# First attention of a fused decoder: rounded inputs scaled by ScalarE, value product and output product one tile sooner, orders set anew

## The reference

```
x = x + attn(layernorm(x))            # layer 0: 16 heads of 32, 4 key/value heads, causal
ln_out = layernorm(x) * ln_w + ln_b   # input of the second attention, for its q, k, v and cross q
y  = clip(ln_out / in_scale, -448, 448)       # in_scale: 512 values for each of the four uses
y  = fp8_e4m3(bf16(y))                        # rounded, used in the next products
```

## Time and profile before

| | us |
|---|---|
| median of 3 runs | 3635.28 (3631.49 to 3635.35) |
| profiled execution, its own time | 3634.33 |
| its span | 3632.6 |
| busy in the span: PE / DVE / ACT / POOL | 3308.4 / 2482.3 / 1673.9 / 855.2 |

### The profile page before, as it was taken

How to read it: one execution, slowest core, us unless ns; L and a number is a source line. 1 busy time by engine, 2 the same in 40 slices (tenths; PEclk the granted TensorE clock), 3 DMA queues, 4 the chain that set the end, 5 groups by cost and what they waited for, 6 DMA issues and landing times. The chain is left out here.

```text
span 3632.6 us, 54605 instructions
## 1 busy us (share of the span) xinstructions
PE 3308.4 (91%) x18088; PEld 2670.3 (74%) x18088; DVE 2482.3 (68%) x6423; ACT 1673.9 (46%) x4003; POOL 855.2 (24%) x915
## 2 busy tenths in 40 slices
PE   5654999997899999999999997999989979998999
PEld 4443887785687787778778775888878757766887
DVE  5997888887566666766666657799765555558333
ACT  5443445444434344444434432688637655542222
POOL 1222444443222222332222223100133310000000
PEclk9877999999999999999999997999999989999999
DMA  6113002002000000110000005899920124333000
GB/s 224 23 23 75 0 0 70 0 0 89 20 21 28 19 21 28 66 43 21 28 19 21 28 0 207 314 407 393 348 80 2 47 105 123 118 102 105 11 10 21
DMA packets 113584, 296.12 MB, mean 82 GB/s; under 512 B 37920, under 2 KB 42016, under 8 KB 107664
## 3 DMA queue, kind: packets, MB, share of 16 engines
q1 hardware_dynamic: 107264, 276.39, 21.6%
q0 software_dynamic: 6160, 17.67, 1.6%
HBM read 251.65 MB, written 41.68 MB: 81 GB/s over the span
## 5 line engine op out<-in xcount | busy, mean ns | idle before, releaser
L40 PE MATMUL bank<-w,cross_ctx_part 128*125 128x512 f32 x1536 | 517.3, 418 | 8.1 <-DVE cross_qn L1091 4.7
L40 PEld LDWEIGHTS bank<-w,cross_ctx_part 128*125 128x125 f32 x1536 | 281.8, 187 | 93.6 <-DVE cross_kn L1091 14.6
L1001 ACT ACTIVATE cross_prob<-bank,cross_neg_max 112x375 f32<-112x375 f32 x256 | 147.0, 574 | 359.2 <-DVE cross_neg_max L1097 359.2
L40 PE MATMUL bank<-w_low,cross_ctx_part 128*125 128x512 f32 x768 | 303.8, 396 | 0.0
L1097 DVE TENSOR_REDUCE cross_neg_max<-bank 112x1 f32<-112x375 f32 x256 | 134.1, 524 | 198.0 <-PE bank L873 195.4
L40 PE MATMUL bank<-moe_wt,moe_zT 128*128 128x448 f32 x1176 | 264.2, 373 | 2.1 <-DVE moe_zT L1727 1.5
L1717 DVE TENSOR_TENSOR moe_wt<-moe_raw,moe_wt 128x1792 fp32r<-128x1792 f32 (+1 forms) x111 | 232.8, 2108 | 21.0 <-ACT moe_wt L1615 20.1
L40 PE MATMUL bank<-w,self_xq 128*112 128x512 f32 x512 | 214.6, 419 | 20.6 <-DVE w_low L596 20.6
L40 PEld LDWEIGHTS bank<-moe_wt,moe_zT 128*128 128x128 f32 x1176 | 215.1, 190 | 17.6 <-issue 1.7
L40 PE MATMUL bank<-mlp_zT,mlp_signs 128*128 128x448 f32 x1024 | 220.6, 368 | 5.6 <-DVE mlp_zT L2407 5.6
L1615 ACT ACTIVATE moe_wt<-moe_raw 128x1792 fp32r<-128x1792 f32 (+1 forms) x111 | 197.0, 1776 | 44.8 <-DMA moe_raw<-in_moe_w 36.1
(11 more groups left out here) (404 smaller groups left out, 8244.5 us busy)
## 6 DMA issues: line engine op xcount, KB each, us to landing
moe_raw<-in_moe_w SPq DMA_DIRECT2D x74, 896.0 KB, 7.8
moe_raw<-in_moe_w SPq DMA_DIRECT2D x37, 1024.0 KB, 8.7
stream<-in_L1f SPq DMA_DIRECT2D x32, 768.0 KB, 8.1
cross_ctx_raw<-in_ctxT SPq DMA_DIRECT2D x32, 750.0 KB, 4.2
wide_ctxT<-in_ctxT SPq DMA_DIRECT2D x16, 750.0 KB, 4.2
wide_ctx_rows<-in_ctx SPq DMA_DIRECT2D x16, 750.0 KB
expert_rows<-a_zeros SPq DMA_DIRECT2D x1, 8960.0 KB, 26.7
moe_zrow<-expert_rows SPq DMA_DIRECT2D x35, 256.0 KB, 8.1
```

The lines of the kernel that those rows point to most:

```text
L40: mm = pe.matmul(out, a, b, start=first and n == 0, stop=last and n == len(pairs) - 1)
L1001: op = act.activation(prob[:, t % SLOTS, i, :], score_bank(t)[0:S, i * NK:(i + 1) * NK], ACT.Exp, bias=neg_max[:, h:h + 1], accum_out=tota ...
```

## The change

GpSimd's multiplication goes, and with it the tile `a_z2T`. In its place two small tables are made once, `in_factor` = ln_w / in_scale and `in_offset` = ln_b / in_scale, and ScalarE writes `a_y` straight out of bank 6, with the table's columns as scale and bias: four operations for each of the four uses, 16 of 128x128 a tile (L2778 after). GpSimd keeps the root. In the same edit the value product and the output product of tile t-1 both run in turn t, the second normalisation takes tile t-2 and the shift tile t-3 (one tile sooner each), the exponentials are cut in two halves, the turn of the scores is parted from the maxima and closes VectorE's turn, and `round_back` is cut in two pairs.

```diff
-            def scale_rows(t):
-                pool.wait_ge(s["z2T_taken"], t + 1)
-                wait(pool, s["shifted"], t - 1)
-                pool.tensor_tensor(y[:, t % 2].rearrange("p v (c t) -> p v c t", c=DC),
-                                   z2T[:, None, :, :].to_broadcast([P, 4, DC, T]),
-                                   in_inverse[:].rearrange("p (v c) -> p v c", c=DC)[:, :, :, None]
-                                   .to_broadcast([P, 4, DC, T]), ALU.mult).then_inc(s["scaled"], 1)
...
+            for part, at in zip(in_affine, (LN_W, LN_W + DC)):
+                dve.tensor_tensor(part[:], in_inverse[:].rearrange("p (v c) -> p v c", c=DC),
+                                  cols[:, None, at:at + DC].to_broadcast([P, 4, DC]), ALU.mult).then_inc(s["products"], 1)
...
-            def take_z2T(t):
+            def scale_inputs(t, v):
                 act.wait_ge(s["z2T_in_psum"], t + 1)
-                wait(act, s["scaled"], t)
+                wait(act, s["shifted"], t - 1)
                 for c in range(DC):
-                    op = act.activation(z2T[:, c, :].rearrange("p (b i) -> p b i", b=B),
+                    op = act.activation(y[:, t % 2, v, c * T:(c + 1) * T].rearrange("p (b i) -> p b i", b=B),
                                         tiled(6)[:, c, :].rearrange("p (i b) -> p b i", b=B), ACT.Identity,
-                                        scale=ln_cols[:, c:c + 1], bias=ln_cols[:, DC + c:DC + c + 1])
+                                        scale=in_affine[0][:, v, c:c + 1], bias=in_affine[1][:, v, c:c + 1])
...
             for t in range(NT + 3):
+                if t >= 3:
+                    transpose_z2(t - 3)
                 if t < NT:
                     scores(t)
+                if 1 <= t < NT + 1:
+                    weigh_values(t - 1)
                 if t + 1 < NT:
                     project_qkv(t + 1)
-                if 2 <= t < NT + 2:
-                    project_out(t - 2)
-                if 1 <= t < NT + 1:
-                    weigh_values(t - 1)
+                if 1 <= t < NT + 1:
+                    project_out(t - 1)
...
             for t in range(NT + 3):
+                if t >= 3:
+                    scale_inputs(t - 3, 1)
+                    scale_inputs(t - 3, 2)
...
-                if t >= 4:
-                    shift(t - 4)
...
+                if 3 <= t < NT + 3:
+                    shift(t - 3)
+                if 1 <= t < NT + 1:
+                    add_out(t - 1)
```

More of the change, by code:

```diff
@@ L2579, in first_layer @@
              "out_low", "y_in_psum", "x_done", "cleared", "stat", "centre", "vareps", "rooted",
-             "z2_ready", "z2T_in_psum", "z2T_taken", "scaled", "clipped", "exponent", "magic", "shifted", "rounded")
+             "z2_ready", "z2T_in_psum", "scaled", "clipped", "exponent", "magic", "shifted", "rounded")
     s = {n: k.sem(f"a0_{n}") for n in names}
@@ L2597, in first_layer @@
         z2 = zeros
-        z2T = sb("z2T", [P, DC, T])
         y = sb("y", [P, 2, 4, DC * T], BF16)
@@ L2652, in root @@
                 pool.tensor_tensor(rstd[:, t:t + 1], ve[:, t:t + 1], k.half[:, 0:1], ALU.pow).then_inc(s["rooted"], 1)
-            root(0)
-            for t in range(1, NT):
+            for t in range(NT):
                 root(t)
-                scale_rows(t - 1)
-            scale_rows(NT - 1)
         @block.tensor
@@ L2679, in transpose_q @@
                 pe.wait_ge(s["q_taken"], t + 1)
-                wait(pe, s["z2T_taken"], t - 4)
+                wait(pe, s["scaled"], 4 * (t - 3))
                 for c in range(DC):
@@ L2719, in transpose_z2 @@
                 pe.wait_ge(s["z2_ready"], t + 1)
-                pe.wait_ge(s["q_ready"], min(t + 5, NT))
-                wait(pe, s["z2T_taken"], t)
+                pe.wait_ge(s["q_ready"], min(t + 4, NT))
+                wait(pe, s["scaled"], 4 * t)
                 for c in range(DC):
@@ L2740, in _ @@
                 if t + 1 < NT:
+                    project_qkv(t + 1)
+                if 1 <= t < NT + 1:
+                    project_out(t - 1)
+                if t + 1 < NT:
                     transpose_q(t + 1)
                     transpose_k(t + 1)
-                if t >= 3:
-                    transpose_z2(t - 3)
                 if t + 2 < NT:
@@ L2769, in take_kT, with exponentials @@
                 act.activation(kT[:], ps[4][:, 0:T], ACT.Copy).then_inc(s["k_ready"], 1)
-            def exponentials(t):
+            def exponentials(t, strips):
                 act.wait_ge(s["minus_max"], t + 1)
-                for r in range(4):
+                for r in strips:
                     for c in range(4):
@@ L2798, in _ @@
             for t in range(NT + 3):
+                if t >= 3:
+                    scale_inputs(t - 3, 1)
+                    scale_inputs(t - 3, 2)
+                if 1 <= t < NT + 1:
+                    out_high(t - 1)
+                if t >= 3:
+                    scale_inputs(t - 3, 3)
                 if t < NT:
-                    exponentials(t)
+                    exponentials(t, (0, 1))
                 if t + 1 < NT:
@@ L2803, in _ @@
                     take_kv(t + 1)
-                if 1 <= t < NT + 1:
-                    out_high(t - 1)
+                if t < NT:
+                    exponentials(t, (2, 3))
                 if t + 1 < NT:
@@ L2814, in _ @@
                     weights.round_high(act, 0, (QS, KS, VS)[t - NT])
+                if 2 <= t < NT + 2:
+                    scale_inputs(t - 2, 0)
         @block.vector
@@ L2874, in shift @@
             def shift(t):
-                dve.wait_ge(s["scaled"], t + 1)
+                dve.wait_ge(s["scaled"], 4 * t + 4)
                 yt = flat(y[:, t % 2])
@@ L2885, in shift, with round_back @@
                 dve.tensor_tensor(flat(shifted[:]), yt, flat(magic[:]), ALU.add).then_inc(s["shifted"], 1)
-            def round_back(t):
+            def round_back(t, parts):
                 dve.wait_ge(s["shifted"], t + 1)
-                for v in range(4):
+                for v in parts:
                     if v < 3:
@@ L2902, in _ @@
             normalise(1)
-            z_low(1)
+            turn_scores(0)
             for t in range(NT + 4):
+                if t + 1 < NT:
+                    z_low(t + 1)
+                if 2 <= t < NT + 2:
+                    measure(t - 2)
+                if t + 2 < NT:
+                    normalise(t + 2)
                 if t < NT:
@@ L2919, in _ @@
                 if 2 <= t < NT + 2:
-                    measure(t - 2)
-                if t >= 4:
-                    round_back(t - 4)
-                if t + 2 < NT:
-                    z_low(t + 2)
+                    normalise_twice(t - 2)
+                if 3 <= t < NT + 3:
+                    shift(t - 3)
+                if 1 <= t < NT + 1:
+                    add_out(t - 1)
+                if t < NT:
+                    turn_probs(t)
+                if 3 <= t < NT + 3:
+                    round_back(t - 3, (0, 1))
+                if t + 1 < NT:
+                    turn_scores(t + 1)
 def raw_and_low(k, ctx, name, shape):
@@ L2944, in decoder @@
             products_of = [k.sb(cross, n, shape, F32) for n, shape in (
-                ("raw_scale", [P, 4, DC]), ("in_inverse", [P, 16]), ("ln_cols", [P, 8]), ("smooth_inverse", [P, 32]),
+                ("raw_scale", [P, 4, DC]), ("in_inverse", [P, 16]), ("smooth_inverse", [P, 32]),
                 ("proj_scale", [P, 1]), ("head_ln", [P, 8]))]
+            products_of.insert(2, [k.sb(cross, n, [P, 4, DC], F32) for n in ("in_factor", "in_offset")])
             x = rows[0:S]
```

32 lines of the change are left out of this document (11 added, 21 removed).

## The result

The changed kernel takes 3576.04 us (median of 4 runs, 3572.41 to 3581.59) against 3633.39 us (4 runs, 3629.47 to 3635.35): a ratio of 0.9845 [0.9828, 0.9862], 57 us less. In a second comparison it was 0.9855 [0.9838, 0.9871]. The profiled execution took 3581.59 us, its span is 3579.9 us.

The account below looks back on a forecast made before the run. VectorE, stalled by GpSimd's product, was taken to set the pace. Opening +0.2, tiles 0 to 3 +4.0, tiles 4 to 12 -41.2 and drain -19.5 gave -56.5, so 3578 us from 3634.3; range 3566 to 3600.

Parts of the forecast that it names:

- The stall and its cause: GpSimd's product, through the shared port pair, costs VectorE 3.4 us a tile of standing still, whichever rounding is there.
- VectorE 13.4 us a tile: VectorE's work in a steady tile once the stall goes: 16.80 - (4.10 - 0.68) = 13.4 us.
- part 4: Value product and output projection one tile sooner: nothing by itself in the steady part; a low clock adds 1.7 us a tile.
- ScalarE 13.2 us: ScalarE's work per steady tile with twelve more scalings at 0.35 us each, 4.2 us, just under VectorE's 13.4.
- The pace: Steady tile of the first attention: from 13.4 us over 15.1 (clock low) to 16.0; 14.1 taken, tiles 4 to 12 giving -41.2.
- The split of the exponentials: Exponentials cut in two halves with the copies of q, k and v between: hides the copies and adds nothing.
- Tiles 0 to 3: Start of the first attention's stage: first three tiles +2.2 us, the next +1.8, together +4.0.
- Drain: End of the first attention's stage: 37.6 us of work and 3.9 of waits, 41.5 instead of 61.0, -19.5.
- ScalarE becomes the bound: Rival: costlier scalings or one 1.5 us wait a tile make the pace 15.6 us, total 3591 us; chance 0.11.
- The root: Rival: roundings on VectorE stand until GpSimd's root is done, at most 0.92 us a tile, 3586 us; chance 0.04.
- The chain: Rival: normalisation, scalings, exponentials and division close in one tile, pace 21.7 us, total 3646 us, slower; chance 0.04.
- The stall stays: Rival: the stall on VectorE has another cause and remains, pace 17.1 us, total 3615 us; chance 0.04.

Follow-up runs that it names:

- the orders alone: The kernel before, GpSimd's product kept, with the new orders of TensorE, ScalarE and VectorE: 3616.54 us, ratio 0.9921, pace 15.55 us.

## Why the prediction was right, and where its sizes were off

The time, 3578 forecast and 3576 measured, is right, and so is the mechanism that carries it. That the two lie 2 us apart is luck: single steps were off by up to 4.5 us in both directions, and the stages behind move by 10 us from one execution to another. The stage's end, 253.6 forecast and 251.7 measured, is the better comparison. The lower end of the forecast doesn't follow from its own sum: a pace of 13.4 in nine tiles gives 3577.8 - 6.3 = 3571.5 us, not 3569.

- **The stall and its cause: right.** The roundings are all near 0.68 us, and the product put back alone makes 4.0 us a tile. "Whichever rounding is there" was right; the orders alone add that turn, low half and measurement pass the product unharmed.
- **VectorE 13.4 us a tile: 13.10 measured.** The lengths of VectorE's operations add up to nearly the same in both kernels, 14.3 us a tile before (without the stall) and 14.2 after. But each operation of a dense queue starts before the last has ended (the roundings of one tile start 0.60 us apart), and such overlaps are 0.9 us a tile before and 1.1 after, which gives 13.4 and 13.1.
- **The orders: where the 2 us of waits went.** The sum goes from 18.76 us a tile to VectorE's 13.4 by taking off the stall, and silently also the 1.96 us in which VectorE didn't work, while part 4 calls the earlier products "worth nothing by itself" in the steady part. With the product gone and the old orders the pace is 15.25, with the new ones 13.60: the orders carry the 1.65 us. Which of them does was not separated.
- **ScalarE 13.2 us: 13.05 measured.** Sixteen scalings in a row take 5.69 us in the drain:

```profile
229.68 5.69 ACT L2778 ACTIVATE a_y<-bank,in_offset,in_factor 128x128 bf16<-128x128 f32 x16 [0.68 <-PE bank L2714]
```

  That is 0.35 us each, as estimated, with two-byte writes; the 0.39 us by the Trainium skill (ScalarE: Activation LUTs, section "What ACT_TABLE_LOAD costs") would, as an estimate from its figure, have made it 6.3. The mean of 497 ns in the groups is the length of one that overlaps the next, not its price.
- **The pace, 14.1 forecast, 13.60 measured: the term that was mis-sized.** Over nine tiles the 0.5 us make the -4.5 by which the steady part beats its forecast. I had put the output product at 10.8 us behind the low half at the worst, with a projection of 7.14 us, and chose a value in the middle. Measured is 6.02, and the product ends 9.5 us behind the low half, when VectorE is ready at 9.3: 0.17 us of wait. "I expect a clock in between" fits the projection's length, 6.02 between 4.45 and 7.14, but not for the reason given: the idle stretch ahead fell to 1.8 us, not 3, and the clock still fell to its lower level in every steady tile.
- **The split of the exponentials "adds nothing": right in the changed kernel, wrong as a rule.** It ties the second half to the projection's end. There it costs nothing, since the exponentials end at 164.72 and the division comes at 165.25, but it takes over as soon as the sum is out of the way. The prediction looked at one way back from the projection, the output product; the sum moved behind the turn showed that there are two.
- **"What is late next is ScalarE, 0.2 us a tile behind VectorE, and then TensorE's clock": the order is wrong.** With a quarter of ScalarE's scaling gone nothing moved. TensorE's clock is first. VectorE is second: the one tile with a projection at full clock and VectorE's whole work took 13.30. ScalarE is third: with the clock held and the normalisation off VectorE, the pace went to 12.99.
- **Tiles 0 to 3: +4.7 instead of +4.0.** The first three took 3.4 us more, not 2.2, and the fourth 1.3 more, not 1.8. VectorE waits there for the output product, 7.6 us in the second turn and 4.2 in the third:

```profile
58.94 0.69 DVE L2852 TENSOR_TENSOR x<-bank,x 128x512 f32<-128x512 f32 x1 [7.61 <-PE bank L40]
...
69.95 0.69 DVE L2852 TENSOR_TENSOR x<-bank,x 128x512 f32<-128x512 f32 x1 [4.19 <-PE bank L40]
```

- **Drain: 42.9 us instead of 41.5.** The work is 37.89 us as forecast (37.6). The waits are 5.0 us instead of 3.9: the scaled inputs are late in the last two tiles, by 1.55 and 1.01 us; 1.27 us lie ahead of the next stage's first work, as before the change, and the rest in smaller gaps:

```profile
235.40 0.69 DVE L2877 TENSOR_SCALAR a_y<-a_y 128x2048 bf16<-128x2048 bf16 x1 [1.55 <-ACT a_y L2778]
...
243.42 0.69 DVE L2877 TENSOR_SCALAR a_y<-a_y 128x2048 bf16<-128x2048 bf16 x1 [1.01 <-ACT a_y L2778]
```

- **The rivals.** "ScalarE becomes the bound" is out by the run with one scaling less. The root costs VectorE nothing, here and where it runs over two roundings. But the prediction read the trace of before as if neither of the two waited: the root took 0.92 us there beside the roundings, against 0.54 beside the maxima alone, so one of them did give way, and by its length it was the root. The chain did not close in one tile. "The stall stays" is out by the roundings.

What stays open: what decides whether the clock falls. In the changed kernel it fell in each steady tile behind 1.8 us of idle time. Behind the same 1.8 us it once stayed up in the run with one scaling less, twice behind 1.86 us in the run with spare products on GpSimd (projections of 4.47 and 4.44 us at 195.16 and 212.74), and once behind 3.05 us with ScalarE's scaling in the old orders (4.45 us at 157.89). So the length of the idle stretch alone doesn't decide. The spare products on TensorE show that filling the stretch holds the clock, in all tiles of two kernels; they don't show how much filling is needed.

## What to carry to other kernels

Move an operation off GpSimd when its SBUF reads lie beside VectorE operations that they hold up (here those with two SBUF inputs, and the normalisation), or place it beside others, and price the move by those operations' stretched times, not by GpSimd's busy share. When two engines come out near the same load, follow every way back from the shared TensorE operation before naming the next bound: a wait of 0.17 us can hide a closed circle, and taking work from either engine then gives nothing. Where TensorE idles a little once a tile and its next long operation is on the circle, look at the granted clock inside that operation.

## What the runs showed of the hardware

- A GpSimd product that reads SBUF holds up VectorE's roundings (two SBUF inputs, 4.67 us for two instead of 1.25) and lengthens its normalisation (1.66 instead of 0.54), but not the turn out of the bank, the low half (bank and SBUF) or the measurement. GpSimd memsets hold up none of the roundings and lengthen one-input operations on two-byte data (1090 ns instead of 686).
- A GpSimd operation of 128x1 beside VectorE's roundings leaves these at 0.68 us and is itself the longer: 1.04 us, against 0.54 beside the maxima.
- TensorE's granted clock fell to 0.50 inside a running projection, in every steady tile of the changed kernel, behind 1.8 us of idle time; in other runs it stayed up behind the same stretch in single tiles. Fourteen products of 0.95 us in all kept it at 1.00 and took the projection from 6.04 to 4.47 us.
- The normalisation of 128x512 takes 0.54 us on VectorE and 2.08 on GpSimd, and there it cost VectorE nothing.
- Two profiled executions of the changed kernel differ by 10 us in span (3579.9 and 3569.6) while the first attention's stage ends within 0.05 us of the same time (251.69 and 251.64): all of the difference lies in the later stages.
